# A vision tower's first stage split into two token halves, with roots and a weight split on GpSimd

## The reference, cut to what matters

```python
# x: [16, 3, 128, 128]; 64 patches of 16 x 16 per image, D = 64
h = patches @ conv_w + conv_b                 # embedding, K = 768
h = layer_norm(h) * ln_w + ln_b + positions
identity = h
h = gelu(h @ w1 + b1) @ w2 + b2               # feed-forward, 256 wide ("ffn1")
q, k, v = split(h @ qkv_w + qkv_b)            # 8 heads of 8
h = softmax(q @ k.T * scale) @ v              # per image and head ("att1")
h = h @ proj_w + proj_b + identity
h = h + gelu(h @ w1 + b1) @ w2 + b2           # "ffn2"
...
# then a norm, single-head attention with a cosine bias, norms, rotary attention,
# and 8 experts of 170 hidden units, of which 2 are used per token, and a last norm
up = rmsnorm(x) * ln2_w @ expert_up           # the split weights up_hi + up_lo
```

## Time and profile before

| | |
|---|---|
| median of 3 runs (lowest, highest) | 129.25 us (129.07, 607.06) |
| profiled execution, its own time | 129.11 us |
| its span on the core | 127.3 us |
| granted TensorE clock, mean | 0.994 |
| busy PE, weight loads, DVE, ACT, POOL | 92%, 61%, 66%, 50%, 13% of the span |

### The profile page before, as it was taken

The page is one execution under the profiler, slowest core; times in us unless marked ns, Lnnn a source line. Parts: engine busy times, 40 slices in busy tenths (PEclk is TensorE's granted clock), DMA queues, the critical chain, the costliest instruction groups (busy, mean ns, idle before and its releaser), DMA issues.

```text
span 127.3 us, 2382 instructions
## 1 busy us (share of the span) xinstructions
PE 117.3 (92%) x935; PEld 77.5 (61%) x935; DVE 83.8 (66%) x180; ACT 63.0 (50%) x124; POOL 16.9 (13%) x40
## 2 busy tenths in 40 slices
PE   5999999969998989999999999799999999999960
PEld 2344564827775854786486987588878873336550
DVE  0000599799999046475878762579689849799862
ACT  4000568975231357535775438567576656363040
POOL 7300009300000000000012003071012320000000
PEclk9999999999999999999999999999999999999997
DMA  4999970000000000000000000000000000000003
GB/s 155 358 392 422 420 319 10 0 0 0 5 0 3 5 0 0 3 0 5 0 0 0 0 5 0 0 5 0 0 0 0 0 0 8 0 0 0 0 0 82
DMA packets 2682, 6.99 MB, mean 55 GB/s; under 512 B 1264, under 2 KB 1392, under 8 KB 2544
## 3 DMA queue, kind: packets, MB, share of 16 engines
q1 hardware_dynamic: 2128, 6.72, 13.5%
q10 hardware_dynamic: 544, 0.13, 0.5%
HBM read 6.59 MB, written 0.26 MB: 54 GB/s over the span
## 4 chain that ended last, share of the span: by engine, by line
PE 68%; DVE 16%; DMA 5%; issue 3%; ACT 3%; POOL 2%; SPq 1%; POOLq 1%; ACTq 0%
PE PS L624 7%; PE PS L625 6%; PE PS L632 5%; DMA shared_x<-x_dram 5%; PE PS L309 4%; DVE top L1134 3%; PE PS L511 3%; PE PS L298 3%; PE PS L287 3%; PE PS L497 3%; DVE shifted L1136 3%; PE PS L395 3%; PE PS L405 2%; PE PS L641 2%; PE PS L317 2%
## 5 line engine op out<-in xcount | busy, mean ns | idle before, releaser
L1295 DVE TENSOR_TENSOR shared_h<-PS,shared_f 128x512 f32<-128x512 f32 x22 | 14.9, 683 | 4.6 <-ACT shared_f L895 4.2
L624 PE MATMUL PS<-xf,up_hi 128*128 128x512 f32 x44 | 17.7, 403 | 0.0
L625 PE MATMUL PS<-xf,up_lo 128*128 128x512 f32 x44 | 17.3, 394 | 0.0
L895 ACT ACTIVATE shared_f<-PS 128x512 f32<-128x512 f32 x22 | 13.0, 596 | 6.1 <-PE PS L625 6.0
L279 PE MATMUL PS<-idle_bf 128*128 128x512 bf16 x39 | 12.0, 427 | 1.3 <-POOL idle_bf L931 1.3
L1134 DVE TENSOR_REDUCE top<-PS 128x8 f32<-128x512 f32 x12 | 8.3, 689 | 2.6 <-PE PS L511 1.2
L800 ACT ACTIVATE probs<-PS 128x512 f32<-128x512 f32 x8 | 4.8, 597 | 10.0 <-PE PS L381 10.0
L624 PEld LDWEIGHTS PS<-xf,up_hi 128*128 128x128 f32 x44 | 8.3, 188 | 2.0
L728 ACT ACT_TABLE_LOAD x7 | 9.0, 1283 | 0.8 <-PEq L1489 0.7
L625 PEld LDWEIGHTS PS<-xf,up_lo 128*128 128x128 f32 x44 | 8.3, 188 | 1.8
L1050 DVE TENSOR_SCALAR kf<-PS,pack_a_sb 128x256 f32<-128x256 f32 x1 | 0.5, 483 | 13.4 <-PE PS L287 13.4
(11 more groups left out here) (193 smaller groups left out, 221.6 us busy)
## 6 DMA issues: line engine op xcount, KB each, us to landing
shared_x<-x_dram SPq DMA_DIRECT2D x6, 544.0 KB, 6.9
up_w<-pack_d_dram SPq DMA_DIRECT2D x1, 1408.0 KB, 12.3
pack_c_sb<-pack_c_dram SPq DMA_DIRECT2D x1, 796.5 KB, 13.0
pack_b_sb<-pack_b_dram SPq DMA_DIRECT2D x1, 455.0 KB, 9.5
down_w<-pack_e_dram SPq DMA_DIRECT2D x1, 352.0 KB, 13.5
pack_a_sb<-pack_a_dram SPq DMA_DIRECT2D x1, 162.0 KB, 8.9
out_dram<-normed SPq DMA_DIRECT2D x2, 64.0 KB, 1.8
out_dram<-normed ACTq DMA_DIRECT2D x2, 64.0 KB, 2.0
```

The costliest lines, as they stand in the source:

```text
L624: mm(up, up_hi[:, at:at + P], moving, start=True, stop=False)
L625: mm(up, up_lo[:, at:at + P], moving, start=False, stop=True).then_inc(sem("up_mm"), 1)
L895: f(gate[:, n % UPBUF, :], PS[:, UP_BANKS[n % UPBUF][0], :], ACT.Silu).then_inc(sem("gated"), 1)
L1295: v.tensor_tensor(hh[:, ch, :, g * HC:(g + 1) * HC], PS[:, UP_BANKS[n % UPBUF][1], :].rearrange("q (s c) -> q s c", s=2), gate[:, n % UPBU ...
```

## The change

1. **Loading.** The conv weights are one transfer of 192 KB; then six chunks of half 0 (256 KB each), packs a and b, and three transfers with two chunks of half 1 each (512 KB).
2. **Order by half.** TensorE does half 0's conv products, centring, norm turn, feed-forward and queries, keys and values; half 1's conv products are spread between them. Half 1's centring comes behind half 0's down product, its turn and `ffn_up` behind half 0's values; its down product stands behind window 0's turn, its queries, keys and values behind window 1's scores. ScalarE and VectorE are reordered to it; VectorE now adds half 1's bias of `f1`, in window 0, and half 1's key bias in window 1. Fillers are fewer and elsewhere. The wait for half 1's queries and keys moves from window 1 to window 2.
3. **Roots.** The first norm's inverse root is made by GpSimd (add, then power -0.5) per half; `Sqrt` with its table load and the reciprocals go.
4. **Weight split.** GpSimd scales the expert up weights in place, casts them to the high part and subtracts: three operations on 128x2816 behind both roots, in place of VectorE's two.

```diff
-        x_sb = shared_x[:, :].rearrange("q (k c) -> q k c", k=KCH)
+        x_sb = shared_x[:, 0:2 * KCH * 2 * HC].rearrange("q (g k c) -> q g k c", g=2, k=KCH)
+        conv_sb = shared_x[:, 2 * KCH * 2 * HC:KCH * XW].rearrange("q (k d) -> q k d", k=KCH)
...
-        CENTRED_BANKS = (6, 1)
+        CENTRED_BANKS = (6, 7)
+        QKV_BANKS = ((0, 1, 4), (6, 7, 5))
+        FFN1_BANKS = (6, 1)
...
+            sp.dma_start(conv_sb, conv.rearrange("q (k d) -> q k d", k=KCH)).then_inc(sem("x_loaded0_0"), 16)
             for k in range(KCH):
-                sp.dma_start(x_sb[:, k, :], x[k]).then_inc(sem(f"x_loaded{k}"), 16)
+                sp.dma_start(x_sb[:, 0, k, :], x[0, k]).then_inc(sem(f"x_loaded0_{k}"), 16)
             sp.dma_start(A[:, :], pack_a).then_inc(sem("pack_a_loaded"), 16)
             sp.dma_start(Bp[:, :], pack_b).then_inc(sem("pack_b_loaded"), 16)
+            for n in range(KCH // 2):
+                sp.dma_start(x_sb[:, 1, 2 * n:2 * n + 2, :], x[1, 2 * n:2 * n + 2].rearrange("k q c -> q k c")).then_inc(sem(f"x_loaded1_{n}"), 16)
             sp.dma_start(up_w[:, :], pack_d).then_inc(sem("up_w_loaded"), 16)
             sp.dma_start(Cp[:, :], pack_c).then_inc(sem("pack_c_loaded"), 16)
             sp.dma_start(down_w[:, :], pack_e).then_inc(sem("down_w_loaded"), 16)
...
+            def conv_products(g, k):
+
+                if g:
+                    pe.wait_ge(sem(f"x_loaded1_{k // 2}"), 16)
+                else:
+                    pe.wait_ge(sem(f"x_loaded0_{k}"), 16 if k else 32)
+                for s in range(2):
+                    m = mm(PS[HALF * s:HALF * s + HALF, 4 + g, 0:HC], conv_sb[:, k, :], x_sb[:, g, k, s * HC:(s + 1) * HC],
+                           start=(k == 0), stop=(k == KCH - 1))
+                if k == KCH - 1:
+                    m.then_inc(sem(f"conv_summed{g}"), 1)
...
+            def ffn_down(name, g, bank):
+
+                for m in range(2):
+                    pe.wait_ge(sem(name + "_gelu"), 2 * g + m + 1)
+                    for s in range(2):
+                        r = slice(HALF * s, HALF * s + HALF)
+                        t = mm(PS[r, bank, 0:HC], b("ff2")[:, m * D:(m + 1) * D],
+                               hidden[:, m, s, g * HC:(g + 1) * HC], start=(m == 0), stop=(m == 1))
+                t.then_inc(sem(name + "_down"), 1)
...
-            pe.wait_ge(sem("idle_made"), 1)
-            stay_awake(7, 7)
-            for k in range(KCH):
-                conv_products(k)
-                if k < KCH - 1:
-                    stay_awake(1, 7)
-
...
-            stay_awake(6, 7)
...
-            pe.wait_ge(sem("proj_bias_made"), 1)
-            stay_awake(1, 7)
-            for g in range(2):
-                ffn_up("ffn1", h0, (0, 2), g)
-            ffn_down("ffn1")
-
-
-            for g in range(2):
-                pe.wait_ge(sem("f1_ready"), g + 1)
-                cols = slice(g * HC, (g + 1) * HC)
-                mm(PS[:, 2 * g, 0:HC], b("wq"), f1[:, cols], start=True, stop=True).then_inc(sem("q1_mm"), 1)
-                mm(PS[:, 2 * g + 1, 0:HC], b("wk"), f1[:, cols], start=True, stop=True).then_inc(sem("k1_mm"), 1)
-                values(f1, b("wv"), D, 4 + g, g).then_inc(sem("v1_mm"), 1)
...
+            def queries_keys_values1(g):
+                q_bank, k_bank, v_bank = QKV_BANKS[g]
+                pe.wait_ge(sem(f"f1_ready{g}"), 1)
+                mm(PS[:, q_bank, 0:HC], b("wq"), half(f1, g), start=True, stop=True).then_inc(sem("q1_mm"), 1)
+                mm(PS[:, k_bank, 0:HC], b("wk"), half(f1, g), start=True, stop=True).then_inc(sem("k1_mm"), 1)
+                values(f1, b("wv"), D, v_bank, g).then_inc(sem("v1_mm"), 1)
...
-                if w == 1:
+                if w == 2:
                     pe.wait_ge(sem("q1_act"), 2)
                     pe.wait_ge(sem("kf_ready"), 2)
...
+            pe.wait_ge(sem("idle_made"), 1)
+            stay_awake(7, 3)
+            for k in range(KCH):
+                conv_products(0, k)
+            stay_awake(1, 3)
+            pe.wait_ge(sem("pack_a_loaded"), 16)
+            centre_embedding(0)
+            pe.wait_ge(sem("pack_b_loaded"), 16)
+            mm(PS[:, 2, 0:1], b("proj"), b("bv"), start=True, stop=True).then_inc(sem("proj_bv"), 1)
+            for k in range(3):
+                stay_awake(1, 3)
+                conv_products(1, k)
+            stay_awake(1, 3)
+            turn_embedding(0)
+            conv_products(1, 3)
+            stay_awake(1, 3)
+            ffn_up("ffn1", h0, (0, 2), 0)
+            conv_products(1, 4)
+            conv_products(1, 5)
+            ffn_down("ffn1", 0, FFN1_BANKS[0])
+            centre_embedding(1)
+            queries_keys_values1(0)
+            stay_awake(2, 3)
+            turn_embedding(1)
+            pe.wait_ge(sem("proj_bias_made"), 1)
+            ffn_up("ffn1", h0, (0, 2), 1)
             pe.wait_ge(sem("vo_set"), 3)
-            for w in range(W8):
+            scores1(0)
+            turn1(0)
+            ffn_down("ffn1", 1, FFN1_BANKS[1])
+            scores1(1)
+            queries_keys_values1(1)
+            for w in range(2, W8):
                 scores1(w)
-                if w == 1:
-                    stay_awake(2, 1)
-                if w >= 1:
-                    turn1(w - 1)
-                if w >= 2:
-                    mix1(w - 2)
+                turn1(w - 1)
+                mix1(w - 2)
...
-            pe.wait_ge(sem("up_split"), 1)
+            pe.wait_ge(sem("up_split"), 3)
...
-            bring_table(ACT.Sqrt)
...
-            roots("ln0", std, 1.0 / D, EPS)
-            bring_table(ACT.Gelu_apprx_tanh)
...
+            gelus("ffn1", (0, 2), 0)
+            act.wait_ge(sem("ffn1_down"), 1)
+            f(half(f1, 0), PS[:, FFN1_BANKS[0], 0:HC], ACT.Identity, bias=b("ff2_b")).then_inc(sem("f1_ready0"), 1)
+            squares0(1)
...
-            queries1(1)
-            bring_table(ACT.Exp)
             act.wait_ge(sem("vo_set"), 3)
             values1(0)
+            gelus("ffn1", (0, 2), 1)
+            bring_table(ACT.Exp)
...
-                if w < len(between):
-                    between[w](1)
+                if w == 0:
+                    queries1(1)
+                if w == 1:
+                    last_slot1(1)
+                if w == 2:
+                    values1(1)
...
+            for g in range(2):
+                at = slice(4 * g, 4 * g + 4)
+                pool.wait_ge(sem("ln0_sq_sum"), g + 1)
+                g_.tensor_scalar(std[:, at], sq_sums[:, at], 1.0 / D, EPS, ALU.mult, ALU.add).then_inc(sem("ln0_above"), 1)
+                pool.wait_ge(sem("ln0_above"), g + 1)
+                g_.tensor_tensor(rstd[:, at], std[:, at], minus_half[:, at], ALU.pow).then_inc(sem("ln0_rstd"), 1)
+
             pool.wait_ge(sem("pack_a_loaded"), 16)
+            pool.wait_ge(sem("up_w_loaded"), 16)
+            g_.tensor_scalar(up_w[:, :], up_w[:, :], a("ln2"), None, ALU.mult).then_inc(sem("up_split"), 1)
+            pool.wait_ge(sem("up_split"), 1)
+            g_.tensor_copy(up_hi[:, :], up_w[:, :]).then_inc(sem("up_split"), 1)
+            pool.wait_ge(sem("up_split"), 2)
+            g_.tensor_tensor(up_lo[:, :], up_w[:, :], up_hi[:, :].bitcast(F32), ALU.subtract).then_inc(sem("up_split"), 1)
...
-            v.tensor_scalar(pos_b[:, :], a("pos"), a("ln_b"), None, ALU.add).then_inc(sem("pos_b_made"), 1)
...
-            ve.wait_ge(sem("up_w_loaded"), 16)
-            v.tensor_scalar(up_hi[:, :], up_w[:, :], a("ln2"), None, ALU.mult).then_inc(sem("up_high"), 1)
-            ve.wait_ge(sem("up_high"), 1)
-            v.scalar_tensor_tensor(out=up_lo[:, :], in0=up_w[:, :], scalar=a("ln2"), in1=up_hi[:, :].bitcast(F32),
-                                   op0=ALU.mult, op1=ALU.subtract).then_inc(sem("up_split"), 1)

...
-            keys1(0)
-            first_slots1(0, range(3))
-            keys1(1)
...
+            ve.wait_ge(sem("pack_a_loaded"), 16)
+            v.tensor_scalar(pos_b[:, :], a("pos"), a("ln_b"), None, ALU.add).then_inc(sem("pos_b_made"), 1)
+            sum_squares("ln0", 0)
+            ve.wait_ge(sem("pack_b_loaded"), 16)
+            ve.wait_ge(sem("proj_bv"), 1)
+            v.tensor_tensor(proj_bias[:, :], PS[:, 2, 0:1], b("bp"), ALU.add).then_inc(sem("proj_bias_made"), 1)
+            normalised0(0)
+            ve.wait_ge(sem("pos_b_made"), 1)
+            place0(0)
+            ve.wait_ge(sem("conv_summed1"), 1)
+            v.tensor_scalar(half(emb, 1), PS[:, 5, 0:HC], a("conv_b"), None, ALU.add).then_inc(sem("emb_ready1"), 1)
+            keys1(0)
+            sum_squares("ln0", 1)
+            first_slots1(0, range(3))
+            normalised0(1)
+            place0(1)
...
                 if w == 0:
                     ve.wait_ge(sem("vo_set"), 3)
                     values1(0)
-                if w in (1, 2):
-                    first_slots1(1, (range(2), range(2, 3))[w - 1])
+                    ve.wait_ge(sem("ffn1_down"), 2)
```

(39 more changed lines are left out.)

76 lines of the change are left out of this document (28 added, 48 removed).

## The result

The changed kernel takes **148.8 us** (median; its four executions went from 146.1 to 150.7), the kernel before 129.1 to 129.3, but for one of 130.6 and an outlier of 607. Executions of one kernel fall into a faster and a slower group, and the ratios, as well as the differences taken from this kernel, compare the faster ones, 146.1 and 147.3 us here: a ratio of **1.135** (95% interval 1.130 to 1.141), so slower by some 17.5 us. The forecast was 135.1 with a range to 139.3. The direction was right; the size was off by a factor of nearly three.

What follows compares the result with a forecast made beforehand. The prediction took TensorE's chain of waits as the bound, with the start of the fourth window's scores deciding: 0.1 + 3.3 + 0.6 + 2.0 = 6.0 us on 129.11 gives 135.1 us, range 130.5 to 139.3.

Steps and rivals of the forecast that it cites:

- Half 0's lead: Half 0, loaded and worked first, has its queries at 18.45 instead of 21.64: 3.2 us ahead.
- parts 2 and 3: Half 0's chain from embedding (9.1) to queries (18.45), then half 1's norm to the first scores (24.6 against 24.46).
- Half 1 behind half 0's keys: On VectorE half 1's sum of squares queues behind half 0's keys; the lead of 3.2 is gone (+0.1).
- Half 1's second part: Half 1's down product, queries, keys and values inside attention delay the fourth window's scores to 33.4 from 30.03: +3.3 in the sum.
- the 0.6: Half 0's three key slots on VectorE and GpSimd's root queue at 20.5 to 22: +0.6, between 0 and 1.0.
- the term of 0.88: First norm's root on GpSimd: sum to scaling takes 1.88 us against 1.00, so 0.88 more for half 0.
- Block at the slot: Half 1's key slot on VectorE in window 1 waits for GpSimd's subtraction: +2.0, bounds 0 and 6.0; no-block rival 0.20.
- the scaling: GpSimd's first split operation on 128x2816, taken as 2.5 us; at the two-input rate 6.5, adding 4.0 (within longer, 0.12).
- The clock: Rival: TensorE's clock falls at a gap before half 1's turn, doubling 4.8 us of products: up to 139.9 (within longer, 0.12).

Runs made afterwards that it cites:

- experiment 1: Changed kernel with GpSimd's weight split begun only after attention's eight shifts: 135.0 us (ratio 1.049).
- experiment 7: experiment 1 plus one dead VectorE operation of 3.15 us behind half 1's first key slot, result not used: 148.2 us.
- experiment 2: experiment 1 plus filler matmuls between half 0's products and ahead of two turns: 133.8 us (ratio 1.038).
- Experiment 8: Kernel before with only its first norm's inverse roots moved to GpSimd: 131.5 us (ratio 1.013).
- experiment 6: experiment 4 plus twelve filler matmuls before the scores of window 4: 138.9 us (ratio 1.070).
- experiment 4: Changed kernel, split early, with the fillers of experiment 2 plus nine before the turn that waits for the blocked slot: 148.0 us (ratio 1.143).
- experiment 5: Changed kernel, split early, with the fillers of experiment 2 and half 1's three key slots made by ScalarE, not VectorE: 134.7 us (ratio 1.042).
- experiment 3: Kernel before with only the weight split moved to GpSimd, ahead of its router work: 138.9 us (ratio 1.074).

## Why the prediction was right or wrong

**Half 0's lead, 3.2 us: held in one execution, not in another.** In the profile of the changed kernel half 0's queries came at 20.27, 1.4 us ahead of before. There the embedding came at 11.05 and not at 9.1: the second chunk's products started only at 6.38, and the clock read 0.50 in 8 to 10.8. Experiments 1 and 7 have the same instructions up to there, and the clock at 1.00. The first had to wait for its chunks and has the embedding at 10.34; the second has it at 9.00, its queries at 18.78 and its first scores at 24.72, where the forecast had 9.1, 18.45 and 24.6. So the chain of parts 2 and 3 is right when the chunks land as in that execution. What it left out is that the chunks' landing and the clock vary from one execution to the next, by up to 2 us at the embedding.

**Half 1 behind half 0's keys: right.** Sum behind keys, scaling 1.84 us behind the sum (forecast 1.88). The first scores are at 27.10 in the changed kernel by the late half 0 and the slow matmuls.

**Half 1's second part, +3.3: right.** Experiment 7's trace, undisturbed up to window 3, has the scores of window 2 at 31.17 (forecast 31.15) and those of the fourth window at 33.22 (33.4). Experiment 2 measured 4.7 for order and roots, where the sum has 3.4 + 0.6 = 4.0. But the 0.6, for half 0's slots beside GpSimd's root, is not in the traces: the three slots took 0.87 us together and the power 1.01, as where no slot is near. Experiment 2's own start was late instead (embedding at 11.43, with fillers between the products). Experiment 8 doesn't test the term of 0.88 for half 0 alone (there it measured 0.90); its 1.6 contain half 1's root in the queue.

**Block at the slot, +2.0 with bounds 0 and 6.0: mechanism right, size off.** One slot lasted 4.04 us, two 5.25, three 10.37, and they ended with GpSimd's instructions; the price is 3.2 to 4.2 us (experiment 6). The mis-sized term is the scaling, 7.41 us (2.63 ns a column) where I took 2.5 by the cast's rate; the bound was 6.5. What the Trainium skill, SBUF - State Buffer, section "Who interferes with whom", says of a VectorE copy or tensor_scalar is borne out by the slots. The line rate for one-input operations in the Trainium skill, GPSIMD Engine Reference, section "Engine selection", agrees with the cast (2.53 us) and not with a tensor_scalar by a column of scalars (7.41 us), so there the measurement decides.

**The clock: the step that failed.** The prediction had it as a rival: "Were the clock to fall, the 4.8 us of products from there to window 2 would about double: up to 139.9". It took the gap before half 1's turn as the only place, and a fall to last until window 2. That fall did come in the profiled execution (0.50 in 25 to 34, with 7.2 us of products in it), and it was the cheap one: 1.1 us between experiments 1 and 2. But the blocked slot makes a second gap, at 38.90 to 41.40, and from it the clock stayed at 0.50 to 68, through six slices in which TensorE never rested. Such a fall is worth 9.1 us (148.0 against 138.9, experiments 4 and 6), more than all terms of my sum together (6.0). I had costed the block as time only, never as a gap on TensorE. With the block in place and the clock held, the time was 138.9, inside the stated range.

**The parts add up for experiment 4**: 4.7 (order and roots, experiment 2) + 0.8 (experiment 5 against 2, cause not shown) + 4.2 (block) + 9.1 (clock) = 18.8, of 18.8 measured (148.0 against 129.2). It must come out, as each part is the difference of two neighbouring runs. The changed kernel is 17.5 slower and lacks the added fillers; that its loss divides in the same way is inferred, not measured.

**What stays open.** Why the clock came back after 3 us in experiment 1, after some 10 in experiment 3 and in the first fall here, but only after 24 to 31 in experiments 4 and 7, no run settles: attention windows ran in all of them. Nor does one settle why two gaps in experiment 7 left it at 1.00.
